# Query and output projections of a cross-attention stacked over heads

## The reference

```python
x = x + self_attention(layernorm(x))              # one head, rotary embedding
xn = layernorm(x)
q = (xn @ Wq).reshape(B, Nq, 16, 64)
k = (context @ Wk).reshape(B, Nk, 16, 64)
v = (context @ Wv).reshape(B, Nk, 16, 64)
scores = einsum('bqhd,bkhd->bhqk', q, k) / sqrt(64)
out = einsum('bhqk,bkhd->bqhd', softmax(scores), v).reshape(B, Nq, 16 * 64)
x = x + out @ Wo + bo
x = x + ffn(layernorm(x))                         # rounded input, ternary weights
```

## Time and profile before

| | |
|---|---|
| median of 3 runs | 1172.28 us (1171.85 to 1172.44) |
| the profiled execution | 1173.88 us, of which the profile's span is 1170.9 us |
| TensorE, products | 1136.2 us busy, 97% of the span |
| TensorE, weight loads | 1047.5 us, 89% |
| VectorE | 934.5 us, 80% |
| ScalarE | 695.5 us, 59% |
| GpSimd | 232.1 us, 20% |
| mean granted clock of TensorE | 0.989 of full speed |

### The profile page before, as it was taken

How to read it: one execution, slowest core, us unless ns; L and a number is a source line. 1 busy time by engine, 2 the same in 40 slices (tenths; PEclk the granted TensorE clock), 3 DMA queues, 4 the chain that set the end, 5 groups by cost and what they waited for, 6 DMA issues and landing times.

```text
span 1170.9 us, 20390 instructions
## 1 busy us (share of the span) xinstructions
PE 1136.2 (97%) x6561; PEld 1047.5 (89%) x6561; DVE 934.5 (80%) x1691; ACT 695.5 (59%) x1001; POOL 232.1 (20%) x228
## 2 busy tenths in 40 slices
PE   6799999999999999999999999999999999999996
PEld 5588999998999899998999989999899999999995
DVE  3698888887888788787978878898788888878645
ACT  1155656656575665756657565665656566575653
POOL 3120130312203022130302213030221303112010
PEclk9799999999999999999999999999999999999998
DMA  7101010010101001010010101001010100100000
GB/s 151 41 1 42 2 41 4 1 42 5 41 3 41 4 2 40 4 41 5 9 36 1 41 5 41 3 2 42 3 41 3 41 3 2 42 2 1 3 1 4
DMA packets 12727, 24.40 MB, mean 21 GB/s; under 512 B 4934, under 2 KB 8654, under 8 KB 12494
## 3 DMA queue, kind: packets, MB, share of 16 engines
q1 hardware_dynamic: 12622, 23.00, 7.4%
HBM read 21.88 MB, written 0.82 MB: 19 GB/s over the span
## 4 chain that ended last, share of the span: by engine, by line
PE 91%; DVE 5%; issue 3%; ACT 1%; DMA 1%; POOL 0%; DVEq 0%; SPq 0%; POOLq 0%; ACTq 0%
PE banks L1086 35%; PE banks L1116 31%; PE banks L940 10%; PE banks L978 4%; PE banks L931 4%; PE banks L960 1%; DVE pr_lo L887 1%; PE banks L1021 1%; DVE maxes L666 1%; PE banks L1011 1%; PE banks L1049 0%; DMA q_hi<-negmaxT 0%; DVE maxes L674 0%; DVE xn L650 0%; ACT banks L617 0%
## 5 line engine op out<-in xcount | busy, mean ns | idle before, releaser
L615 ACT ACTIVATE pr_hi<-banks 128x800 fp32r<-128x800 f32 x384 | 322.4, 840 | 393.4 <-PE banks L1086 393.4
L666 DVE TENSOR_REDUCE maxes<-banks 128x1 f32<-128x482 f32 x585 | 370.4, 653 | 57.6 <-PE banks L940 53.8
L887 DVE TENSOR_TENSOR pr_lo<-banks,pr_hi 128x800 fp32r<-128x800 f32 x320 | 315.0, 985 | 56.8 <-ACT banks L617 56.4
L617 ACT ACTIVATE banks<-banks 128x800 f32<-128x800 f32 x384 | 319.8, 833 | 0.0
L940 PE MATMUL banks<-cT_hi,q_hi 96*128 96x482 f32 x585 | 223.6, 382 | 1.4 <-DVE maxes L666 1.4
L1086 PE MATMUL banks<-q_hi,cT_hi 97*128 97x400 f32 x768 | 216.7, 363 | 8.3 <-DMA q_hi<-negmaxT 7.4
L1116 PE MATMUL banks<-pr_hi,cN_hi 128*97 128x400 f32 x768 | 214.2, 346 | 0.1
L1086 PE MATMUL banks<-q_hi,cT_lo 96*128 96x400 f32 x768 | 208.5, 352 | 0.0
L1086 PE MATMUL banks<-q_lo,cT_hi 96*128 96x400 f32 x768 | 204.4, 347 | 0.0
L1116 PE MATMUL banks<-pr_hi,cN_lo 128*96 128x400 f32 x704 | 190.6, 344 | 0.0
L1116 PE MATMUL banks<-pr_lo,cN_hi 128*97 128x400 f32 x704 | 190.6, 344 | 0.0
(11 more groups left out here) (116 smaller groups left out, 887.6 us busy)
## 6 DMA issues: line engine op xcount, KB each, us to landing
cT_raw<-in_ctxT SPq DMA_DIRECT2D x16, 568.5 KB
cN_raw<-in_ctx SPq DMA_DIRECT2D x16, 528.0 KB
out<-result SPq DMA_DIRECT2D x16, 50.0 KB
X<-in_x SPq DMA_DIRECT2D x1, 700.0 KB
cN_raw<-in_ctx_last SPq DMA_DIRECT2D x16, 40.5 KB
wqT<-in_wqT SPq DMA_DIRECT2D x1, 512.0 KB, 5.4
wo<-in_wo SPq DMA_DIRECT2D x1, 512.0 KB, 13.2
wkT<-in_wkT SPq DMA_DIRECT2D x1, 384.0 KB, 7.2
```

Of the source, the lines that this page charges most:

```text
L615: nc.scalar.activation(pr_hi[:, s % RING, :].rearrange("p (a q) -> p a q", a=2), pair, ACT.Exp, scale=float(DH) ** -0.5).then_inc(hi_done, 1)
L617: nc.scalar.activation(pair, pair, ACT.Exp, scale=float(DH) ** -0.5).then_inc(exp_done, 1)
L666: nc.vector.tensor_reduce(maxes[:, t, p:p + 1], here[:, 0:PW], AX.X, ALU.max).then_inc(misc_free, 1)
L887: nc.vector.tensor_tensor(pr_lo[:, s % RING, :].rearrange("p (a q) -> p a q", a=2), banks[:, slot:slot + 2, 0:BLK], pr_hi[:, s % RING, :]. ...
```

## The change

The 96 rows of the four heads that share a position in the four blocks are stacked to 384 rows, which are 3 groups of 128 (`KB`). M is stored so that a product takes 128 columns across heads: the query projection becomes 3 fills of 4 products with 128 stationary columns, in place of 4 fills of 4 products with 96. ScalarE and VectorE write the high and the low part into stacked tiles, qs_hi and qs_lo (128 x 400 for each fill), and SyncE moves pieces of 32, 64 or 96 rows from there into q_hi and q_lo (`move_q`); the table STACKED lists the six pieces as (block, first row, rows, group, first row in the group). The "max" products wait for the landings of the pieces of their block. The "q" fills stand at steps 0, 1 and 2.

For the output, SyncE moves o_sb into a stacked tile o_st, and the reciprocals go through a row in DRAM from which six transfers spread them over r_st; GpSimd multiplies o_st by r_st and no longer broadcasts. G is moved once into a stacked G_st. The projection "y" is 12 products with G_st stationary (128 columns) and o_st moving (100), at step 11; its result is transposed, so VectorE copies it to yT, and a new fill "yT" at step 12 transposes it back. The last batch keeps its products by head. The reciprocals are taken at step 5.

```diff
@@ constants
+PARTED = [1, 2, 2, 1]
+STACKED = [(0, 0, 96, 0, 0), (1, 0, 32, 0, 96), (1, 32, 64, 1, 0), (2, 0, 64, 1, 64), (2, 64, 32, 2, 0),
+           (3, 0, 96, 2, 32)]
-    QB = H // 4
+    KB = 4 * DC // P
@@ tiles
-        M = sb("M", [D, H, DC])
+        M = sb("M", [D, 4, 4 * DC])
+        qs_hi = sb("qs_hi", [P, KB, BLK], F32R)
+        qs_lo = sb("qs_lo", [P, KB, BLK], F32R)
-        rrow = sb("rrow", [1, Q])
-        rball = sb("rball", [DC, Q])
+        rrow = nc.dram_tensor("rrow", [Q], F32).ap()
+        yT = sb("yT", [D, S])
+        G_st = sb("G_st", [P, KB, 4, D])
+        o_st = sb("o_st", [P, KB, BLK])
+        r_st = sb("r_st", [P, KB, BLK])
@@ the steps of the fills
-        BETWEEN = {0: ("q", 2), 1: ("q", 3), 2: ("AO", 1), 4: ("T2", 1)}
+        BETWEEN = {0: ("q", 2), 2: ("AO", 1), 4: ("T2", 1)}
-        LATE = ("q", "y")
-        for j in range(QB):
-            AT[(0, 3, 5, 8)[j]].append(("q", j, 1))
-        AT[12].append(("y", 0, -1))
+        LATE = ("q", "y", "yT")
+        for j in range(KB):
+            AT[j].append(("q", j, 1))
+        AT[11].append(("y", 0, -1))
+        AT[12].append(("yT", 0, -1))
@@ SyncE
-            def move_sums(n, par):
+            def move_q(n, par, use, j):
+
+                sp.wait_ge(qhi_done, n * KB + j + 1)
+                for i, row, rows, k, to in STACKED:
+                    if k == j:
+                        sp.dma_start(q_hi[par][row:row + rows, i * BLK:(i + 1) * BLK].bitcast(F32),
+                                     qs_hi[to:to + rows, k, :].bitcast(F32)).then_inc(qhi_in_s[i], 16)
+                sp.wait_ge(misc_free, use + 1)
+                for i, row, rows, k, to in STACKED:
+                    if k == j:
+                        sp.dma_start(q_lo[par][row:row + rows, i * BLK:(i + 1) * BLK].bitcast(F32),
+                                     qs_lo[to:to + rows, k, :].bitcast(F32)).then_inc(qlo_in_s, 16)
+
+            def move_out(n, par, y_use):
 
                 sp.wait_ge(o_evac, NB * (n + 1))
                 sp.dma_start(sums[:, :], o_sb[par][DC:DC + 1, :].rearrange("p (h s) -> p h s", h=H)).then_inc(sums_in_s, 16)
+                if y_use is not None:
+                    sp.wait_ge(misc_ready, y_use + 1)
+                for i, row, rows, k, to in STACKED:
+                    sp.dma_start(o_st[to:to + rows, k, :],
+                                 o_sb[par][row:row + rows, i * BLK:(i + 1) * BLK]).then_inc(ost_in_s, 16)
+
+            def move_sums(n):
+
                 sp.wait_ge(recip_done, n + 1)
-                sp.dma_start(rrow[:, :].rearrange("p (h s) -> p h s", h=H), rsums[:, :]).then_inc(rrow_in_s, 16)
+                sp.dma_start(rrow.rearrange("(h s) -> h s", h=H), rsums[:, :]).then_inc(rrow_in_s, 16)
+                sp.wait_ge(rrow_in_s, (n + 1) * 16)
+                for i, row, rows, k, to in STACKED:
+                    sp.dma_start(r_st[to:to + rows, k, :],
+                                 rrow[i * BLK:(i + 1) * BLK].rearrange("(a q) -> a q", a=1).to_broadcast([rows, BLK])).then_inc(rst_in_s, 16)
@@ SyncE, in each body
+                if present(b, 1):
+                    move_q(b + 1, 1 - par, use_of(b, "q"), 0)
+                if present(b, -1):
+                    move_out(b - 1, 1 - par, use_of(b - 1, "y") if present(b, -2) else None)
+                if present(b, 1):
+                    for j in range(1, KB):
+                        move_q(b + 1, 1 - par, use_of(b, "q", j), j)
...
                 if present(b, -1):
-                    move_sums(b - 1, 1 - par)
+                    move_sums(b - 1)
@@ GpSimd, normalize
-                if isinstance(n, int):
-                    pool.wait_ge(rrow_in_s, (n + 1) * 16)
-                order.link(nc.gpsimd.partition_broadcast(rball[:, :], rrow[:, :]))
-                nc.gpsimd.tensor_tensor(out=o_sb[par][0:DC, :], in0=o_sb[par][0:DC, :], in1=rball[:, :],
+                pool.wait_ge(ost_in_s, (n + 1) * 16 * len(STACKED))
+                pool.wait_ge(rst_in_s, (n + 1) * 16 * len(STACKED))
+                nc.gpsimd.tensor_tensor(out=o_st[:, :, :], in0=o_st[:, :, :], in1=r_st[:, :, :],
                                         op=ALU.mult).then_inc(on_done, 1)
@@ ScalarE, high_q
-                nc.scalar.activation(q_hi[par][0:DC, j * BLK:(j + 1) * BLK], banks[0:DC, bank, 0:BLK],
-                                     ACT.Copy).then_inc(qhi_done, 1)
+                if j == 0:
+                    for i in range(4):
+                        at_least(act, qhi_in_s[i], n * 16 * PARTED[i])
+                nc.scalar.activation(qs_hi[:, j, :], banks[:, bank, 0:BLK], ACT.Copy).then_inc(qhi_done, 1)
@@ VectorE
-                    dve.wait_ge(qhi_done, n * QB + j + 1)
-                    nc.vector.tensor_tensor(q_lo[par][:, j * BLK:(j + 1) * BLK], here[0:DC, 0:BLK],
-                                            q_hi[par][0:DC, j * BLK:(j + 1) * BLK].bitcast(F32),
+                    dve.wait_ge(qhi_done, n * KB + j + 1)
+                    if j == 0:
+                        at_least(dve, qlo_in_s, n * 16 * len(STACKED))
+                    nc.vector.tensor_tensor(qs_lo[:, j, :], here[:, 0:BLK], qs_hi[:, j, :].bitcast(F32),
                                             ALU.subtract).then_inc(misc_free, 1)
...
                 elif what == "y":
+                    nc.vector.tensor_copy(yT[:, :], here[:, 0:S]).then_inc(misc_free, 1)
+                elif what == "yT":
...
-                    if s == 3 and present(b, -1):
+                    if s == 5 and present(b, -1):
@@ TensorE
-                    for i in range(4):
-                        h = 4 * j + i
-                        mm = nc.tensor.matmul(here[0:DC, i * S:(i + 1) * S], M[:, h, :], x2T[par][:, :],
+                    for g in range(4):
+                        mm = nc.tensor.matmul(here[:, g * S:(g + 1) * S], M[:, g, j * P:(j + 1) * P], x2T[par][:, :],
                                               start=True, stop=True)
...
-                        pe.wait_ge(qhi_done, n * QB + bank_of[t] + 1)
+                        pe.wait_ge(qhi_in_s[bank_of[t]], (n + 1) * 16 * PARTED[bank_of[t]])
...
-                    for h in range(H):
-                        mm = nc.tensor.matmul(here[0:S, 0:D], o_sb[par][0:DC, h * S:(h + 1) * S], G[:, h, :],
-                                              start=(h == 0), stop=(h == H - 1))
+                    for h in range(4):
+                        for k in range(KB):
+                            mm = nc.tensor.matmul(here[:, 0:S], G_st[:, k, h, :], o_st[:, k, h * S:(h + 1) * S],
+                                                  start=(h == 0 and k == 0), stop=(h == 3 and k == KB - 1))
+                elif what == "yT":
+                    mm = nc.tensor.transpose(here[0:S, 0:D], yT[:, :], ident[:, :])
...
+                    pe.wait_ge(qlo_in_s, (b + 1) * 16 * len(STACKED))
```

More of the change, by code:

```diff
@@ L297, in body_uses, with use_of @@
             return found
-        def use_of(b, wanted):
-            return next(use for step in body_uses(b) for what, _, _, use, _ in step if what == wanted)
+        def use_of(b, wanted, number=0):
+            return next(use for step in body_uses(b) for what, j, _, use, _ in step if (what, j) == (wanted, number))
         def batches(eng, body):
@@ L412, in store @@
                 sp.dma_start(out[n, :, :], result[par][:, :]).then_inc(out_s, 16)
+            for j in range(KB):
+                move_q(0, 0, START.index(("q", j)), j)
             split_done(0)
@@ L418, in _ @@
                          negmaxT[0:FIRST, :].bitcast(F32)).then_inc(row_a_in_s, 16)
+            sp.wait_ge(g_done, 4)
+            for i, row, rows, k, to in STACKED:
+                sp.dma_start(G_st[to:to + rows, k, :, :], G[row:row + rows, 4 * i:4 * i + 4, :]).then_inc(gst_in_s, 16)
             def body(b, par):
@@ L871, in body @@
                             consume(b + away, par if away % 2 == 0 else 1 - par, what, j, use, bank)
-                    y_before = s > 0 and "y" in [what for what, *_ in at[s - 1]]
+                    y_before = s > 0 and "yT" in [what for what, *_ in at[s - 1]]
                     if s == 0 or "AO" in whats or y_before:
```

18 lines of the change are left out of this document (13 added, 5 removed).

## The result

| | before | after |
|---|---|---|
| median | 1172.36 us (4 runs) | 1238.26 us (4 runs, 1237.59 to 1238.60) |
| ratio | | 1.0558, 95% interval 1.0544 to 1.0573 |
| span of the profiled execution | 1170.9 us | 1236.5 us |

The change makes the kernel 5.6% slower. The direction was forecast, the size was not: 1191 us, with a range to 1206.

The account below looks back on a forecast made before the run. TensorE, busy for 97% of the span, bounds the kernel. On the profiled 1173.88 us, -14.0 + 33.0 - 2.3 + 3.0 - 0.8 = +18.9 gives 1192.8; against the median 1172.28 it is 1191 us, range 1179 to 1206.

Parts of the forecast that it names:

- the products: Query and output projections on TensorE: fewer, wider products, less an added transpose, gain 0.93 us a body, 14.0 us in all.
- The rival of free width: Both projections: 128 stationary columns cost the 86 ns of 96, so the kernel gets faster, 1164.5 us; chance 5%.
- the wait: First maximum product of the next batch waits for q's transfer: 2.2 us in each of 15 bodies, 33 us.
- a term for late transfers: q's transfer into q_hi comes late in some bodies, as the maxima's transfer did: 3 us added.
- what is given back: Weight loads no longer meet VectorE's late subtraction around step 3, 2.3 us off; shorter start, 0.8 us off.
- the clock falls at the wait: Behind q's wait TensorE drops to 1.2 GHz, half of 17 us lost 15 times: about 1315 us; chance 3%.
- The part on the output projection: Output projection: reciprocals, transfers and GpSimd's multiply finish about 5 us before the products need them; failing by 1 us, 1206 us.
- the cover of each edit that it costed at nothing: Other engines' work lies beside TensorE's, and q_hi's other banks land by step 5, before step 7 reads them: no cost.
- The nearly hidden wait: First maximum product: TensorE arrives a block later or landing takes 1.2 us, nothing measured, 1170 to 1175 us; chance 5%.
- the second wait at the output projection: Output projection, moved up a step, waits for the reciprocals' chain; at 1 us a body, 1206 us; chance 4%.

Follow-up runs that it names:

- the run with 96 columns: Changed kernel with maxima later, output projection at step 12, transpose at 13, and 96 stationary columns for q from batch 1 on: 1155.47 us, ratio 0.9846.
- the run with one row: Kernel before, plus a one-row copy of q_hi's block 0 to an unread tile, whose landing the first maximum product awaits: 1193.43 us, ratio 1.0179.
- yT at step 13: Changed kernel with maximum products later and only the transpose back moved from step 12 to 13: 1192.28 us, ratio 1.0167.
- products by head: Changed kernel, maxima later, output projection by head at step 13, a constant transpose at step 12, normalization left out of the output: 1192.53 us, ratio 1.0166.
- the last: Changed kernel with maximum products later, output projection at step 12, transpose back at 13 and VectorE's normalization at 14: 1164.27 us, ratio 0.9931.
- y a step later: Changed kernel with the output projection at step 12 instead of 11 and the transpose back at step 13: 1226.74 us, ratio 1.0435.
- two copies: Kernel before, plus two successive copies of q_hi's block 0 (96 rows), the first maximum product waiting for the second: 1262.0 us, ratio 1.0757.
- the later maxima: Changed kernel with the first two maximum products of step 1 moved to steps 2 to 4, all transfers kept: 1173.35 us, ratio 1.0006.

## Why the prediction was wrong in size

**Right: the products.** Forecast 0.93 us a body, measured 0.82. Passes cost 0.100 us with 128 stationary columns and 0.078 with 96 (forecast 109 and 86 ns, from the chain). The rival of free width falls, directly by the run with 96 columns. With the rule that it cited from the Trainium skill (TensorE: Matmul & The Clock Gate, LDWEIGHTS), time by the number of columns, the trace agrees: 96/128 of the columns, 78% of the time.

**Right: the wait.** Forecast 2.2 us behind two score pairs, 15 times, and 3 us for late transfers; measured 2.12 in body 0, 2.49 in eleven bodies and 2.26 to 2.36 in three, none late. In sum 36.4 us for 36. That the total fits so well is in part luck: a term for late transfers that didn't come (3 us) made up for a landing put too short. The landing has a median of 2.4 us, for which I took 2.2; the fit of the Trainium skill (DMA: Bandwidth & Descriptors, Anatomy of one DMA) gave 2.35, and with it the trace agrees.

**Wrong: what is given back.** I took off 2.3 us for VectorE's late subtractions and 0.8 at the start. The waits of weight loads for these subtractions do go in the three kernels that have only an added wait; in the changed kernel they are 6.8 us in 15 places, and the loop's edge rose by 2.1 us. The first scores start at 56.96 us where before they started at 56.79: the start waits for other things than q's products, and body 0 adds another 3.6 us, 2.1 of them its wait.

**The step that failed: the clock.** I had it as a rival, "the clock falls at the wait", at 3%, and its mechanism is what happened, in 13 bodies of 14. Two things were wrong in it. The chance: I had bounds on either side of 2.2 us, 3.58 us with a fall and about 1 us without, and no row between, yet I left the kernel at full clock with 97%. By those two rows it was open. The price: I took the stretch at the start, 17 us low, for the pattern, and got 1315 (half of 17 us, 15 times, on 1191 is 1318). But there TensorE is idle for 3 of the first 10.6 us, and in the loop it is busy at once; the low stretch behind a wait lasts 3.4 us, in three of the 13 cases 6.8, and 3.4 us cost 1.7 at most. So the rival seemed to forecast something absurdly large, which helped to dismiss it. At 2 us a body it gives 1191 + 29 = 1220, and the range would have had to reach there. The Trainium skill (TensorE: Matmul & The Clock Gate, HAM oscillation) prices such a stretch at half its length; the trace agrees roughly: the bodies with and without a fall give 1.5 to 1.6 us for 3.4.

**The step that was missing: cover.** The part on the output projection asked what y waits for (the reciprocals; that was right: GpSimd's multiply ended 4 us ahead, and y had no idle time), but not what had been waiting behind y. Moving 3.4 us of products out of step 12 uncovered the chain from aggregate to root to xn, 0.81 us a body, 10.5 us. The prediction named the cover of each edit that it costed at nothing, and never the cover that the moved block had given to others. Together: 18.9 forecast, plus 28.9 (clock in the loop), 10.5 (cover), 2.3 + 2.1 (subtractions, edge), 1.7 (products), 0.4 (wait), 0.8 (start) and 1.6 (body 0 beyond its wait) is 67.2, against 65.6 measured.

**The other rivals.** The nearly hidden wait and the second wait at the output projection did not happen; that y would need the maxima's place in VectorE's queue was in none of them.

## What to carry to other kernels

A wait in front of a saturated TensorE as long as those that brought the clock down here (1.95 us in 8 of 14 bodies, 2.49 in 13) is to be priced twice, once for its length and once, at half the length of the low stretch at most, for the clock behind it, and above all avoided: here one edit of the order that put other work between the transfer and its first reader was worth 65 us, while the cheaper products are worth 12. When a block of work is moved, ask what stood beside it: the chains of the other engines that it covered are now due at the same time as before and have nothing to hide behind. With both waits gone the stacked kernel is 1.1% faster than the one before (1159.78 us), so the idea was sound and its placement wasn't.

## What the hardware showed that I had not expected

- The fall of the clock has a soft edge. Behind waits of 1.37 to 1.50 us it never came (14 bodies of the run with one row), behind 1.69 us in 2 of 13 (yT at step 13), behind 1.95 to 2.10 in 8 of 14, behind 2.49 in 13 of 14, behind 4.20 always. One fall came behind less, two waits of 0.65 and 1.14 us that stood 1.8 us apart (products by head, at 242.46). At the loop's edge falls came behind waits of 1.7 to 1.9 us in five of the runs and not behind one of 2.07 in the last. What decides within one kernel, where the waits are alike, these runs don't show.
- A low stretch lasted 3.4 us or 6.8, though TensorE was busy without a gap from its first microsecond on (727.50 to 730.90 above). In bodies 1 to 14 it was 6.8 in the twelve cases in which the fall came 0.27 us or more before the wait was over (three in the changed kernel, three with y a step later, six with two copies), and 3.4 in all others.
- A granted clock of 1.00 can be a missing record. The view gives 1.00 for 46 to 56 us in the changed kernel and 0.50 in the one before, but the trace of the first has no record of the clock ahead of 62 us, and its products take as long there: the first scores' pairs are 0.81 and 0.66 us from the next start (56.96, 57.77), before 0.80 and 0.67 (56.79, 57.59), against 0.45 and 0.37 at the full clock. Mean clocks of whole runs that differ by 0.01 say little for the same reason.
- Twenty-four more transfers a body, of 50 to 150 KB, beside everything else, cost TensorE nothing that could be measured: with the later maxima the span is 1.1 us below the kernel before, and the cheaper products (-12.3), the wait of step 13 (+10.5) and the loop's edge (+0.9) give -0.9.
